# An FFN without loops: down products of one tile between the gate and up products of the next

## What is computed

```python
h  = layernorm(x2)                                  # x2: [2048, 512]
p  = h @ (values(gate_up) * scale per group).T      # [2048, 2 * 1408]
y  = (silu(p[:, :1408]) * p[:, 1408:]) @ down.T     # [2048, 512]
out = x2 + y / sqrt(mean(y * y) + 1e-6)
```

## Time and profile before

| | |
|---|---|
| median of three runs | 1453.63 us (1452.6 to 1454.66) |
| the profiled execution | 1456.01 us, span 1454.2 us |
| granted clock of TensorE, mean | 0.98 |
| busy: TensorE (PE) | 1374.0 us, 94% |
| busy: VectorE (DVE) | 982.8 us, 68% |
| busy: ScalarE (ACT) | 512.3 us, 35% |
| busy: GpSimd (POOL) | 445.6 us, 31% |
| the FFN, from its first transpose to the end | 1149.89 to 1454.2 us |

### The profile page before, as it was taken

The page is one execution under the profiler, slowest core; times in us unless marked ns, Lnnn a source line. Parts: engine busy times, 40 slices in busy tenths (PEclk is TensorE's granted clock), DMA queues, the critical chain, the costliest instruction groups (busy, mean ns, idle before and its releaser), DMA issues. The chain is left out here.

```text
span 1454.2 us, 25225 instructions
## 1 busy us (share of the span) xinstructions
PE 1374.0 (94%) x8788; PEld 803.0 (55%) x8788; DVE 982.8 (68%) x2187; ACT 512.3 (35%) x1221; POOL 445.6 (31%) x306
## 2 busy tenths in 40 slices
PE   8999999958899989999899999999989999999997
PEld 6666666425466646666566666664434434343433
DVE  6344344447777777777777767765869796969693
ACT  3222222322333333333333343330001483838281
POOL 0000000003333333333333333331402292929292
PEclk9999999988999999999899999999999999999999
DMA  8555555321100110001100020027852000000000
GB/s 327 212 206 200 207 192 190 140 105 58 59 29 29 34 68 29 29 29 43 58 29 29 14 88 29 29 94 194 237 158 92 1 2 29 0 29 0 29 1 30
DMA packets 59552, 122.01 MB, mean 84 GB/s; under 512 B 4328, under 2 KB 37864, under 8 KB 52840
## 3 DMA queue, kind: packets, MB, share of 16 engines
q1 hardware_dynamic: 59496, 121.27, 24.6%
HBM read 96.09 MB, written 25.17 MB: 83 GB/s over the span
## 5 line engine op out<-in xcount | busy, mean ns | idle before, releaser
L923 POOL TENSOR_TENSOR hd_rotated<-hd_products 64x512 f32<-64x512 f32 x64 | 112.8, 1763 | 718.6 <-DVE hd_products L1124 718.6
L183 PE MATMUL psum<-hd_xt_hi,hqk_hi 128*128 128x512 f16 x512 | 198.5, 388 | 4.9 <-DVE hd_xt_lo L1094 4.9
L184 PE MATMUL psum<-hd_xt_lo,hqk_hi 128*128 128x512 f16 x512 | 197.8, 386 | 0.0
L185 PE MATMUL psum<-hd_xt_hi,hqk_lo 128*128 128x512 f16 x512 | 197.3, 385 | 0.0
L1438 POOL TENSOR_TENSOR ff_part<-ff_part 128x512 f32<-128x512 f32 x88 | 127.5, 1464 | 99.7 <-DVE ff_part L1565 99.3
L183 PE MATMUL psum<-hd_wv_hi,hd_xt_hi 128*128 (+1 forms) x512 | 140.3, 274 | 5.0 <-DVE hd_wv_lo L1099 5.0
L1467 PE MATMUL psum<-ff_xt_hi,gu 128*128 128x512 f16 x352 | 133.9, 380 | 9.2 <-DVE ff_part L1565 3.3
L184 PE MATMUL psum<-hd_wv_lo,hd_xt_hi 128*128 (+1 forms) x512 | 140.3, 274 | 0.0
L185 PE MATMUL psum<-hd_wv_hi,hd_xt_lo 128*128 (+1 forms) x512 | 140.2, 274 | 0.0
L1468 PE MATMUL psum<-ff_xt_lo,gu 128*128 128x512 f16 x352 | 133.4, 379 | 0.0
L1565 DVE SCALAR_TENSOR_TENSOR ff_part<-psum,gu_scale,ff_part 128x512 f32<-128x512 f32 x176 | 119.8, 738 | 6.5 <-ACT ff_part L1515 3.6
(11 more groups left out here) (168 smaller groups left out, 2815.9 us busy)
## 6 DMA issues: line engine op xcount, KB each, us to landing
xa_kv_t<-in_ctx_t_dram SPq DMA_DIRECT2D x16, 1024.0 KB, 4.9
xa_kv<-in_ctx_dram SPq DMA_DIRECT2D x16, 1024.0 KB, 4.8
w_rows<-in_head_weights_dram SPq DMA_DIRECT2D x12, 1024.0 KB, 6.9
z_scratch<-hd_z_hi SPq DMA_DIRECT2D x32, 256.0 KB, 2.2
z_scratch<-hd_z_lo SPq DMA_DIRECT2D x32, 256.0 KB, 2.3
w_rows<-z_scratch SPq DMA_DIRECT2D x8, 1024.0 KB, 8.0
hqk_lo<-z_scratch SPq DMA_DIRECT2D x8, 1024.0 KB, 8.0
xn<-in_x_dram SPq DMA_DIRECT2D x8, 512.0 KB, 3.7
```

Of the source, the lines that this page charges most:

```text
L183: pe.matmul(out, lh, rh, start=(first and i == 0), stop=False)
L184: pe.matmul(out, lh, rl, start=False, stop=False)
L185: last = pe.matmul(out, ll, rh, start=False, stop=(final and i == k - 1))
L923: pool.tensor_tensor(rotated[0:HALF, w, 0, :], products[0:HALF, w, 0, :], products[0:HALF, w, 2, :], ALU.subtract)
```

## The change

In the FFN every loop is written out. TensorE's program becomes: turn and gate/up of tile 0; then for each tile t some of its down jobs alone, the turn of tile t+1, and the gate/up units of t+1 with the other down jobs of t between them. A job is (row block i, hidden block b), three matmuls. Of 44 jobs of a tile, in the order shown, 22 run alone behind tile 0, 9 behind tiles 1 and 2, and all behind tile 3. Beside tile 1's gate/up the 22 others stand behind units 3 to 17, one or two each. Beside tiles 2 and 3 there are 35: three behind each of units 0 to 3, one behind unit 4, two behind each of units 8 to 18.

Six banks go round for the turned x and the groups; banks 6 and 7 hold results in turn (row blocks 0 and 2 in bank 6, 1 and 3 in bank 7; in the last tile 2 and 3 lie in banks 0 and 1). `h_hi` and `h_lo` have two buffers, for even and odd tiles. The squares go to `junk`, not to `gate`. The result steps (`finish`) take two row blocks at a time, and so do the stores. In VectorE's program a finish of the tile before stands behind the scale-and-add of a certain even unit: unit 20 for row blocks 2 and 3, unit 6 for row blocks 0 and 1 in tiles 2 and 3; for tile 0's row blocks 0 and 1 it stands ahead of tile 1's second halves. The layernorm has three parts now (statistics, inverse root, output). Tile 1's comes as before behind tile 0's last gate product; those of tiles 2 and 3 are put behind the gate products of blocks 0, 1 and 2 of the tile before. The four tiny transposes ahead of tile 0 (L1457) are gone, and gate/up's first unit waits for each turned bank by itself.

The diff, cut to its core:

```diff
-def layernorm(dve, t, src, dst, stat, step, ready, by_code=False, parts=(1, 2), blocks=TT):
+def layernorm(dve, t, src, dst, stat, step, ready, by_code=False, parts=(1, 2, 3), blocks=TT):
...
+        early, late = range(FB - 2), range(FB - 2, FB)
+        jobs = [(i, b) for i in (0, 1) for b in early] + [(i, b) for i in (0, 1) for b in late] + [(i, b) for i in (2, 3) for b in range(FB)]
+        pair = len(jobs) // 2
+        def jobs_at(t):
+            if t == NT - 1:
+                return [jobs], None
+            first = pair if t == 0 else len(early)
+            per_unit = [0] * UNITS
+            if first < pair:
+                for n in range(pair - first):
+                    per_unit[n // 3] += 1
+                start = -(-(pair - first) // 3) + 3
+                spaces = [start + n // 2 for n in range(pair)]
+            else:
+                spaces = [3 + n * (UNITS - 7) // pair for n in range(pair)]
+            assert max(spaces) <= UNITS - 4
+            for u in spaces:
+                per_unit[u] += 1
...
+            return [jobs[0:first]], split
...
+        ROTATE = 6
+        in_order = [("x", 0, k) for k in range(KD)]
+        for t in range(NT):
+            in_order += [("p", t, u, g) for u in range(UNITS) for g in range(KD)]
+            if t < NT - 1:
+                in_order += [("x", t + 1, k) for k in range(KD)]
+        placed = [(unit, n % ROTATE) for n, unit in enumerate(in_order)]
+        placed += [(("y", t, i), i - 2 if t == NT - 1 and i >= 2 else ROTATE + i % 2) for t in range(NT) for i in range(TT)]
+        banks = Banks(nc, ctx, "ff", placed, [])
...
+            def gate_up(t, u):
+                first = u % 2 * FF + u // 2 * P
+                for g in range(KD):
+                    unit = ("p", t, u, g)
+                    if u == 0:
+                        banks.wait_moved(pe, None, ("x", t, g))
+                    banks.wait_room(pe, None, unit)
+                    pe.matmul(psum_of(unit), gu[:, g, first:first + P], xt_hi[:, g, :], start=True, stop=False)
+                    banks.fills(pe.matmul(psum_of(unit), gu[:, g, first:first + P], xt_lo[:, g, :], start=False, stop=True), None, unit)
+            def down(t, i, b):
+                unit = ("y", t, i)
+                h_hi, h_lo = h_pairs[t % 2]
+                if b == 0:
+                    banks.wait_room(pe, None, unit)
+                if i == 0:
+                    pe.wait_ge(h_lo_done, t * FB + b + 1)
...
+            turn_xn(0)
+            for u in range(UNITS):
+                gate_up(0, u)
+            for t in range(NT):
+                (alone,), beside = jobs_at(t)
+                for i, b in alone:
+                    down(t, i, b)
+                if beside is not None:
+                    turn_xn(t + 1)
+                    for u in range(UNITS):
+                        gate_up(t + 1, u)
+                        for i, b in beside[u]:
+                            down(t, i, b)
...
+            for t in range(NT):
+                if t:
+                    for i in range(TT):
+                        if block_done_before(t - 1, i) == -1:
+                            square(t - 1, i)
+                first_halves(t)
+                for b in range(FB + 2):
...
+                    if t and b < FB:
+                        for i in range(TT):
+                            if block_done_before(t - 1, i) in range(max(2 * b - 1, 0), 2 * b + 1):
+                                square(t - 1, i)
+            for i in range(TT):
+                square(NT - 1, i)
...
+            for t in range(NT):
+                if t and block_done_before(t - 1, 1) == -1:
+                    finish(t - 1, 0)
+                second_halves(t)
                 for b in range(FB + 1):
+                    for u in (2 * b, 2 * b + 1) if b < FB else ():
+                        scale_and_add(t, u)
+                        if t:
+                            for p in range(2):
+                                if u % 2 == 0 and block_done_before(t - 1, 2 * p + 1) in range(max(u - 3, 0), u - 1):
+                                    finish(t - 1, p)
                     if b:
+                        gated(t, b - 1)
+                    if 0 < t < NT - 1 and b in (1, 2, 3):
+                        normalize(t + 1, (b,))
+                if t == 0:
+                    normalize(1, (1, 2, 3))
+            for p in range(2):
+                finish(NT - 1, p)
```

More of the change, by code:

```diff
@@ L157, in layernorm @@
             done(dve.bn_aggr(stat["meanvar"][:, i, :], stat["six"][:, i, :]), wait=(i == blocks - 1))
-    if 2 not in parts:
-        return
[L160 to L165, removed]
+    now = {k: v[:, 0:blocks] for k, v in stat.items() if k not in ("six", "meanvar")}
+    y = now["y"]
+    if 2 in parts:
+        n[0] = 2 * blocks
+        done(dve.tensor_scalar(now["var"], stat["meanvar"][:, 0:blocks, 1], LN_EPS, None, ALU.add))
+        inverse_root(dve, now, done)
+        done(dve.tensor_scalar(y, y, XS, None, ALU.mult))
+        assert n[0] == steps
+    if 3 not in parts:
+        return
     for i in range(blocks):
@@ L1116, in on_the_side @@
                 if not last_tile:
[L1117 removed]
+                    layernorm(dve, t, xn, xn, stat, ln_step, xn_ready, parts=(2, 3))
             def rotate(s, w):
@@ new lines, in first_halves, with scale_groups @@
+                    banks.wait_filled(act, None, ("x", t, k))
+                    act.activation(xt_hi[:, k, :], psum_of(("x", t, k)), ACT.Copy).then_inc(xt_hi_done, 1)
+            def scale_groups(t, u):
+                m = t * UNITS + u
+                if m >= SLOTS:
+                    act.wait_ge(hidden_done if u % 2 == 0 else silu_done, (m - SLOTS) // 2 + 1)
+                for g in range(2):
+                    unit = ("p", t, u, g)
+                    banks.wait_filled(act, None, unit)
+                    banks.moves(act.activation(part[:, slot_of(t, u), g, :], psum_of(unit), ACT.Copy, scale=scale_of(u, g)), None, unit)
@@ new lines, in gated, with normalize @@
+            def gated(t, b):
+                n = t * FB + b
+                dve.wait_ge(summed, t * UNITS + 2 * b + 2)
+                if n >= 2:
+                    dve.wait_ge(h_lo_done, n - 1)
+                dve.wait_ge(silu_done, n + 1)
+                dve.scalar_tensor_tensor(hidden[:, n % 2, :], part[:, slot_of(t, 2 * b + 1), 0, :], HS / XS, gate[:, n % 2, :],
+                                         ALU.mult, ALU.mult).then_inc(hidden_done, 1)
+            def normalize(t, parts):
+                if 1 in parts:
+                    for k in range(KD):
+                        banks.wait_filled(dve, None, ("x", t - 1, k))
+                layernorm(dve, t - 1, x2[:, t * TT:(t + 1) * TT, :], xn, stat, ln_step, xn_ready, by_code=True, parts=parts)
```

255 lines of the change are left out of this document (99 added, 156 removed).

## The result

The changed kernel takes 1483.92 us, the median of four runs; one of them was disturbed (5021.73 us), and without it the median is 1482.85 (1481.75 to 1485.0), which I use below. The kernel before takes 1453.12. The ratio is 1.0202 [1.0186, 1.0219], some 30 us more. The forecast was 1465.6 with a range to 1477: slower was right, and the size was 17 us short. The profiled execution took 1481.75 for a span of 1479.8.

A forecast was written before the change was run, and what follows sets the result against it. VectorE and GpSimd bound gate/up, TensorE the down stage. TensorE's idle goes from 21.3 to 33.8 us (+12.5); with -2.0 at the start and +1.5 at the end, +12.0 gives 1465.6 us, range 1452 to 1477.

The forecast's parts named there:

- Seam: Between tiles 0 and 1: TensorE waits 1.4 for the layernorm, then for second halves behind a finish; idle 4.0 us.
- rival 4: ScalarE reloads tables around each square, two loads for each of five finishes: 12.8 us more at most, 1478; 3%.
- tail: Behind the last matmul: the last finish handles two row blocks, one result step more and a larger store; +1.5 us.
- Tile 1's middle: Gate/up beside 22 jobs: layernorm on VectorE delays banks, TensorE waits 1.1 at unit 8 and 0.6 at unit 10; 2 us.
- Tile 2's middle: Layernorm and finish meet units with few jobs: waits at units 7, 8 and job (2, 0), largest term; 9 us.
- The end waits: Ends of tiles 1 to 3: next down product waits for row block 2's bank behind finish; 3.3, 3.4, 3.4 us.
- I take about one operation per chain: Each of seven small-step VectorE chains loses about one GpSimd operation, since GpSimd has at most two queued there.
- The price of 2.4: By the skill page's mutual exclusion, each small-step VectorE chain could lose a GpSimd add and a subtraction, 2.4 us.
- The clock: TensorE's clock may drop behind idle waits, costing about 2.5 us each; nothing taken, bound 3 x 2.5 = 7.5 us.
- VectorE absorbs it: Units 6 to 10 and 20: layernorm, finishes and holds fit TensorE's longer blocks, only fixed terms left; 1442.5 us, 12%.
- Only the end waits vanish: At the ends of tiles 1 to 3 finish runs sooner: -10 us, 1455.5, no measurable change; 13%.
- Holds and clock at full: GpSimd's delays of VectorE chains and TensorE's clock loss: +8 and +7.5 us at most, middle 1473; 17%.

The follow-up runs named there:

- The last experiment: GpSimd's adds cut to 8 of 512 columns in the written-out old order with bank sets changing roles from tile to tile: 1430.63 us (one run).
- all of it together: Changed kernel with layernorm parts under jobs, row blocks 2 and 3 finished separately, finishes and jobs moved, 13 lone jobs behind tiles 1 and 2: 1475.18 us.
- 1441: Kernel before with loops written out, bank sets changing roles, hidden blocks 0 to 7 first, no down product beside gate/up: 1441.19 us, ratio 0.9912.
- the seam's experiment: Changed kernel with tile 1's second halves ahead of the finish of tile 0's row blocks 0 and 1 on VectorE: 1480.8 us, ratio 1.0197.
- the kernel with short adds: Changed kernel with GpSimd's adds of the two sums cut to 8 of 512 columns: 1459.98 us (one run).

## Why the prediction was right and wrong

**What bounds the kernel** was read rightly: two stages with two limits, and a total of 21.3 to be won. The last experiment shows that GpSimd's adds are part of what makes the limit.

**Start**: 2.04 behind the turn, forecast 2.06. **Seam**: 0.71 + 2.88 by starts, forecast 1.4 + 2.6; gate/up of tile 1 started 64.8 behind the first turn, by the forecast 64.46. **Tile 3**: 2.67, forecast 2. **The stores and squares** cost nothing; one table load is left in the FFN, so rival 4 is refuted and the loads did go with the loops' heads. The **tail** grew by 0.5, not 1.5.

**Tile 1's middle**: 1.19 + 2.09 = 3.3, forecast 2. Part 2 of the layernorm was reckoned at 2.58 and took 4.56, from 1226.95 to 1231.51, with GpSimd beside its first two steps (VectorE's timeline of the changed kernel):

```profile
1226.95 1.24 DVE L162 TENSOR_SCALAR ln_var<-ln_meanvar 128x4 f32<-128x4 f32 x1
1228.22 1.08 DVE L125 TENSOR_SCALAR ln_half<-ln_var 128x4 int32<-128x4 int32 x1
```

**Tile 2's middle**: 3.67 + 1.46 + 1.25 = 6.4, forecast 9: the places are right (unit 8, then the result bank), the walk 2.6 too long.

**The end waits**: 4.63 three times = 13.9, forecast 10.1. Of the 1.3 that each is longer, half is the hold: the step "I take about one operation per chain" put it at 1, and the chain met a subtraction and an add, 1.6 in sum. The other half is the walk: without the holds the wait is 3.04 and not 2.4, as the finish begins 0.1 ahead of TensorE's asking and not 0.8. The held steps at 1269.68 and 1270.43 are `tensor_scalar` with a single input, two numbers per partition. The Trainium skill ("SBUF — State Buffer", "Who interferes with whom") names not only VectorE instructions with two SBUF inputs, as I had it, but also `tensor_scalar` when it runs in a mode that takes both of VectorE's port pairs. The trace agrees with that. The price of 2.4 that I named by the page was too large, because the subtraction was half over when the chain met it (0.7 of 1.16 was left). An unforeseen wait of 0.76 stands in tile 0's lone jobs, where job (0, 8) asks for GpSimd's `h_lo`.

Together the idle time is 38.1, where the forecast had 33.8: off by 4.3, within the bounds that the prediction gave the holds.

**The clock** is where it failed. The step is: "Mine of 3.3 lie between and nearer to 4.61 than I like; I take nothing, the bound is 3 x 2.5 = 7.5." Both halves were wrong. Taking nothing was a choice for one end of a gap (1.66 kept the clock, 4.61 lost it) with no row in between. And the bound counted only the end waits, while the seam, tile 1's middle, tile 2's (twice) and tile 3's lost the clock too: eight stretches and 14.6 us, where the same rows allowed a price for each wait above 1.66. With 14.6 more and 4.3 of idle, less 1.0 at the tail, the forecast's +12.0 becomes 29.9, what length and tail measure (29.4 + 0.5).

**The rivals.** VectorE absorbs it: against it stand the waits in the middles. Only the end waits vanish: they are the largest. Holds and clock at full was the mechanism that came, and its top, 1481, still 2 too low for the reason above.

**What stays open**: the order of "all of it together" has waits that I did not trace one by one, so whether an interleaved order can beat 1441 on this chip is not settled; the edits tried leave it at 1470 to 1475. Moving GpSimd's adds to another engine, or its subtraction ahead of its adds, wasn't tried.

## What to carry to other kernels

Before slack on one engine is filled, ask what makes it: here two engines at their limit made it, and the interleaved order made TensorE wait for those same two at more places. A wait on TensorE costs its length and may cost a slow stretch behind it (1.5 to 2.7 us here); price both for each wait in the walk, not for the longest alone. And look first at what small placements give: which bank was moved long ago, and whether the loop is needed.

## What the runs showed of the hardware

**The clock falls after short waits.** Matmuls at the level of 1.2 GHz (0.61 to 0.63, starts 0.427 apart) followed idle times of 4.47 (three times), 3.51, 2.67 and 2.51 in the changed kernel. Two shorter ones were followed by them as well, each with another wait close ahead: 1.93, with 1.02 ended 7.7 us before, and 1.04, with 3.51 ended 4.6 us before. 1.66 and 2.01 (the seam's experiment) left the clock, and so did one of 3.50 in the kernel "all of it together", behind which the granted clock is 1.00 from 1305.6 to 1311.0 (TensorE's timeline):

```profile
1305.61 0.39 PE L1514 MATMUL psum<-ff_xt_hi,gu 128*128 128x512 f16 x1 [3.50 <-DVE ff_part L1613]
```

The same wait did both in the kernel with short adds: after 2.88 at 1266.27 eight matmuls were slow from 0.6 us on, after 2.89 at 1347.27 and at 1421.50 none. I counted the waits in the FFNs of all traces: of 44 between 1.9 and 3.5 us 30 had a slow stretch behind them and 14 had none, and all 16 above 3.5 us had one. So in between the length alone doesn't decide, and what does is open. A stretch of the changed kernel held 7 to 13 slow matmuls and cost 1.5 to 2.7 us. The prediction's only row of a lost clock was 4.61.

**Small VectorE steps are held as long as large ones, but not all of them.** 0.16 to 0.17 becomes 1.08 to 1.24 beside one GpSimd operation of 1.16 to 1.27. 12 steps in one go lost 1.6. Steps with two inputs are held on one number per partition too. A `tensor_scalar`, with its one input, is held on two or four numbers per partition and not on one. The run that finishes row block 2 alone has both kinds side by side (VectorE's timeline, then GpSimd's):

```profile
1269.68 0.14 DVE L1641 TENSOR_SCALAR ff_rms_var<-ff_squares 128x1 f32<-128x1 f32 x1
1269.86 0.15 DVE L125 TENSOR_SCALAR ff_rms_half<-ff_rms_var 128x1 int32<-128x1 int32 x1
...
1270.46 1.19 DVE L129 SCALAR_TENSOR_TENSOR ff_rms_y<-ff_rms_y,ff_rms_var 128x1 f32<-128x1 f32 x1
```

```profile
1269.26 1.15 POOL L1494 TENSOR_TENSOR wo_lo<-ff_hidden,wo_hi 128x512 f16<-128x512 f32 x1
```

At the same place the changed kernel's steps of 128x2 took 0.72 and 1.19. Over all traces, of the `tensor_scalar` steps that began with over 0.3 us of a GpSimd operation left, all 79 on two or four numbers were held, and none of the 46 on one.

**Writing the loops out made tiles shorter**: 1.0 us in tiles 1 and 2, 0.5 in tile 3 and nothing in tile 0, found by writing them out alone. Whether it is the loop as such or the table loads that went with it is open.
